# Sandwich layer on eight cores: the PSUM eviction of y moved from VectorE to ScalarE, and the first FFN block placed between the last transposes

## The reference

```python
x = u
# diagonal state space model, 32 complex states
Bu  = einsum('bld,nd->bln', layernorm(x), B_bar)
xs  = scan(a=Lam_bar, b=Bu)                  # over the 4096 tokens
y   = 2*real(einsum('bln,dn->bld', xs, C)) + D * layernorm(x)
x   = x + layernorm(y)
# quantised feed-forward, hidden size 5632, uint8 weights minus 128, times a scale
h   = silu(layernorm(x) @ Wg.T) * (layernorm(x) @ Wu.T)
out = x + layernorm(h @ Wd.T)
```

## Time and profile before

| | us |
|---|---|
| median of 3 runs | 2667.18 |
| lowest, highest run | 2664.41, 2741.41 |
| the profiled execution, time | 2664.85 |
| the profiled execution, span of its slowest core (core 5) | 2663.3 |
| spans of the eight cores | 2651.8 to 2663.3 |

### The profile page before, as it was taken

How to read it: one execution, slowest core, us unless ns; L and a number is a source line. 1 busy time by engine, 2 the same in 40 slices (tenths; PEclk the granted TensorE clock), 3 DMA queues, 4 the chain that set the end, 5 groups by cost and what they waited for, 6 DMA issues and landing times.

```text
span 2663.3 us, 26373 instructions; the slowest of 8 cores (2651.8 to 2663.3 us)
## 1 busy us (share of the span) xinstructions
PE 2111.1 (79%) x10668; PEld 1024.1 (38%) x10668; DVE 758.5 (28%) x1412; ACT 497.2 (19%) x465; POOL 126.6 (5%) x238
## 2 busy tenths in 40 slices
PE   1466224332999999999978979999999999998980
PEld 0455212221444444444433434444444444443330
DVE  5666686764111111111011012221222221011114
ACT  1454202233100000000412210000000003122201
POOL 1000000001000000000000000000000000000000
PEclk9877655565999999999988989999999999999995
DMA  2344013335122122223222122333333323121216
GB/s 64 132 153 159 16 63 127 126 127 157 65 79 79 67 77 79 80 79 148 109 97 93 48 107 80 126 114 123 127 127 127 122 84 134 44 95 73 80 49 221
DMA packets 51579, 270.20 MB, mean 101 GB/s; under 512 B 6146, under 2 KB 6146, under 8 KB 34818
## 3 DMA queue, kind: packets, MB, share of 16 engines
q0 software_dynamic: 30528, 146.81, 15.6%
q1 hardware_dynamic: 20356, 117.51, 12.8%
q10 hardware_dynamic: 576, 4.19, 0.4%
HBM read 151.58 MB, written 47.71 MB: 75 GB/s over the span
## 4 chain that ended last, share of the span: by engine, by line
PE 76%; DVE 13%; DMA 4%; issue 4%; ACT 2%; DVEq 0%; SPq 0%; POOL 0%; ACTq 0%; POOLq 0%
PE pA L751 12%; PE pA L788 12%; PE pA L761 11%; PE pB L751 11%; PE pB L788 6%; PE pD L761 6%; PE pC L761 6%; PE pD L788 3%; PE pC L788 3%; DVE arena L936 2%; DVE arena L1095 1%; DVE arena L1082 1%; DMA out<-arena 1%; DVE arena L1076 1%; DMA ysp<-arena 1%
## 5 line engine op out<-in xcount | busy, mean ns | idle before, releaser
L788 PE MATMUL pA<-arena 128*128 128x512 bf16 x1408 | 373.8, 386 | 22.4 <-DVE arena L1187 18.9
L751 PE MATMUL pA<-arena 128*128 128x512 bf16 x1408 | 316.3, 383 | 17.8 <-DMA arena<-wu 13.4
L761 PE MATMUL pA<-arena 128*128 128x512 bf16 x1408 | 311.1, 379 | 0.0
L751 PE MATMUL pB<-arena 128*128 128x512 bf16 x1408 | 311.1, 379 | 0.0
L788 PE MATMUL pB<-arena 128*128 128x512 bf16 x704 | 215.8, 387 | 30.7 <-DVE arena L1187 30.7
L788 PEld LDWEIGHTS pA<-arena 128*128 128x128 bf16 x1408 | 139.4, 99 | 199.6 <-issue 41.7
L751 PEld LDWEIGHTS pA<-arena 128*128 128x128 bf16 x1408 | 138.6, 99 | 188.4 <-issue 25.4
L1151 DVE TENSOR_SCALAR arena<-pA,arena 128x512 bf16<-128x512 f32 x88 | 62.0, 746 | 500.0 <-PE pA L761 500.0
L700 PE MATMUL pA<-arena 32*128 32x512 bf16 x64 | 39.4, 616 | 207.3 <-DVE arena L1095 136.7
L751 PEld LDWEIGHTS pB<-arena 128*128 128x128 bf16 x1408 | 138.0, 98 | 165.9
L761 PEld LDWEIGHTS pA<-arena 128*128 128x128 bf16 x1408 | 137.8, 98 | 166.1
(11 more groups left out here) (202 smaller groups left out, 1714.2 us busy)
## 6 DMA issues: line engine op xcount, KB each, us to landing
arena<-wg POOLq DMA_DIRECT2D x88, 512.0 KB, 3.5
arena<-wu POOLq DMA_DIRECT2D x88, 512.0 KB, 4.3
arena<-u SPq DMA_DIRECT2D x32, 1024.0 KB, 6.0
arena<-wd POOLq DMA_DIRECT2D x16, 1408.0 KB, 5.9
arena<-wd POOLq DMA_DIRECT2D x8, 2816.0 KB, 10.0
arena<-uprev SPq DMA_DIRECT2D x16, 1024.0 KB, 5.7
x1sp<-arena SPq DMA_DIRECT2D x16, 1024.0 KB, 4.7
arena<-x1sp SPq DMA_DIRECT2D x16, 1024.0 KB, 10.0
```

The costliest lines, as they stand in the source:

```text
L751: C.inc(t.matmul(gps[tg], wgbuf[par][:, kt * 128:(kt + 1) * 128], xnt[:, kt * TH + tg * 512: kt * TH + (tg + 1) * 512], start=(kt == 0), s ...
L761: C.inc(t.matmul(ups[tg], wubuf[par][:, kt * 128:(kt + 1) * 128], xnt[:, kt * TH + tg * 512: kt * TH + (tg + 1) * 512], start=(kt == 0), s ...
L788: C.inc(t.matmul(PS2[ti], Hbuf[:, hb * TH + ti * 128: hb * TH + (ti + 1) * 128], wsrc[:, wof * 512:(wof + 1) * 512], start=(hb == 0), stop ...
```

## The change

Three edits.

- ACT copies `pA` to `ybuf_p`, at the head of its slot, and DVE only waits for that (`yev_k`) ahead of the y statistics. The copy waited for `ln2_(k-2)` before; it waits for `x1_(k-2)` now.
- POOL issues the weight loads of the first two blocks ahead of the spill stores. Each waits for the y matmuls that read the SBUF range below it.
- PE does block hb 0 of X 0 in four groups of 16 matmuls, one behind each of the transposes of tiles 11 to 14. Block hb 1 is the first in the loop over blocks.

```diff
--- before.py
+++ after.py
@@ -417,6 +417,15 @@
                                   channel_multiplier=1), "g",
                   mark=("g_ddiag" if kd == 15 else None))
 
+        for hb in (0, 1):
+            wkey = "d_w" if hb % 2 == 0 else "d_w2"
+            C.wait(g, f"ymm_{11 + hb}")
+            C.inc(g.dma_start(wgbuf[hb][:, :], d_in["wg"][hb, :, :]),
+                  wkey, 16)
+            C.wait(g, f"ymm_{13 + hb}")
+            C.inc(g.dma_start(wubuf[hb][:, :], d_in["wu"][hb, :, :]),
+                  wkey, 16, mark=f"wconv_0_{hb}")
+
         for k in range(8):
             C.wait(g, f"xnevv_{k + 8}")
             C.wait(g, f"xnevs_{k + 8}")
@@ -429,12 +438,11 @@
 
         for X in range(2):
             for hb in range(HB):
+                if X == 0 and hb < 2:
+                    continue
                 par = hb % 2
-                if X == 0 and hb < 2:
-                    C.wait(g, "yev_15")
-                else:
-                    pX, phb = (X, hb - 2) if hb >= 2 else (0, HB - 2 + hb)
-                    C.wait(g, f"s1mm_{pX}_{phb}")
+                pX, phb = (X, hb - 2) if hb >= 2 else (0, HB - 2 + hb)
+                C.wait(g, f"s1mm_{pX}_{phb}")
                 wkey = "d_w" if par == 0 else "d_w2"
                 C.inc(g.dma_start(wgbuf[par][:, :], d_in["wg"][hb, :, :]),
                       wkey, 16)
@@ -533,6 +541,15 @@
                            bias=c_Tlnr), "s", mark="s_rpow")
         for sl in range(NT + 5):
             k = sl - 1
+            if 0 <= k < NT:
+                C.wait(s, f"ymm_{k}")
+                if k >= 2:
+                    C.wait(s, f"x1_{k-2}")
+                for gq in range(4):
+                    C.inc(s.activation(
+                        ybuf_p[k % 2][:, 512 * gq:512 * (gq + 1)],
+                        pA[:, 512 * gq:512 * (gq + 1)], AF.Copy), "s",
+                        mark=(f"yev_{k}" if gq == 3 else None))
             if 0 <= k < NT:
                 C.wait(s, f"yaggr_{k}")
                 C.inc(s.activation(sdy_p[k % 2], mvy_p[k % 2][:, 1:2],
@@ -714,17 +731,39 @@
                       mark=(f"ymm_{i}" if kd == 15 else None))
             if i >= 5:
                 xntr_block(i - 5)
-        for k in range(NT - 5, NT):
-            xntr_block(k)
+        def s1q0(buf, ps, tg, mk):
+            for kt in range(16):
+                C.inc(t.matmul(ps,
+                               buf[:, kt * 128:(kt + 1) * 128],
+                               xnt[:, kt * TH + tg * 512:
+                                   kt * TH + (tg + 1) * 512],
+                               start=(kt == 0), stop=(kt == 15)), "t",
+                      mark=(mk if kt == 15 else None))
+
+        xntr_block(11)
+        C.wait(t, "wconv_0_0")
+        C.wait(t, "yev_15")
+        C.wait(t, "xnevv_3")
+        C.wait(t, "xnevs_3")
+        s1q0(wgbuf[0], pA[:, 0:512], 0, None)
+        xntr_block(12)
+        C.wait(t, "xnevv_7")
+        C.wait(t, "xnevs_7")
+        s1q0(wgbuf[0], pA[:, 512:1024], 1, "gmm_0_0")
+        xntr_block(13)
+        s1q0(wubuf[0], pA[:, 1024:1536], 0, None)
+        xntr_block(14)
+        s1q0(wubuf[0], pA[:, 1536:2048], 1, "s1mm_0_0")
+        xntr_block(15)
 
         PS2 = [pA[:, 0:512], pA[:, 512:1024], pA[:, 1024:1536],
                pA[:, 1536:2048], pB[:, 0:512], pB[:, 512:1024], pC, pD]
         for X in range(2):
             for hb in range(HB):
+                if X == 0 and hb == 0:
+                    continue
                 par = hb % 2
                 C.wait(t, f"wconv_{X}_{hb}")
-                if X == 0 and hb == 0:
-                    C.wait(t, "yev_15")
                 if X == 0 and hb == 1:
                     C.wait(t, "xnevv_15")
                     C.wait(t, "xnevs_15")
@@ -1087,15 +1126,7 @@
                       mark=f"x1aggr_{k}")
             k = sl - 1
             if 0 <= k < NT:
-                C.wait(v, f"ymm_{k}")
-                if k >= 2:
-                    C.wait(v, f"ln2_{k-2}")
-                C.selfwait(v, "v")
-                for gq in range(4):
-                    C.inc(v.tensor_copy(
-                        ybuf_p[k % 2][:, 512 * gq:512 * (gq + 1)],
-                        pA[:, 512 * gq:512 * (gq + 1)]), "v",
-                        mark=(f"yev_{k}" if gq == 3 else None))
+                C.wait(v, f"yev_{k}")
                 C.selfwait(v, "v")
                 for gq in range(4):
                     C.inc(v.bn_stats(
```

## The result

The changed kernel takes 2599.88 us (median of 8 runs, 2597.14 to 2603.54). The ratio to the kernel before is 0.9753, 95% interval 0.9739 to 0.9768: 2.5% faster, where 2604.3 us and 2.36% were forecast.

What follows compares the result with a forecast made beforehand. A ring of waits in the tile loop, 17.33 us a turn, was taken as the bound. 8.0 + 33.8 - 4.7 + 25.25 - 0.6 - 1.2 = 60.5 us saved from 2664.85 gave 2604.3 us, range 2593 to 2626.

Steps and rivals of the forecast that it cites:

- first slots: Start of the tile loop, up to tile 4's eviction: shorter without the wait behind x1 statistics, gain 8.0 us.
- eleven turns: Tile loop from there to the last y eviction: 191.1 us becomes 157.3 at 14.3 a turn, gain 33.8.
- tail: Transposes, evictions and spill stores after the last y eviction: first ACT steps start later, loss 0.6 us.
- half clock at the start of hb 1: PE's clock may have dropped before block hb 1: cost between 0 and 2.5 us, 1.2 taken.
- E: Time of the y eviction on ACT, four f32 PSUM copies: 2.12 to 2.54 us, 2.35 taken.
- The ring: Tile loop's ring of waits: PE, normalise on ACT, add on DVE, evict on ACT; 17.33 us falls to 14.3 a turn.
- The spill: Tile 8's spill queues on POOL behind the early weight loads and delays tile 9's evictions: loss 4.7 us once.
- the rival that had them exposed: Tail: the four matmul blocks between the last transposes stay uncovered, costing 27.3 us, total 2632; chance 0.10.
- Clock up in the loop: Rival: PE keeps its clock in the tile loop, the statistics ring of 13.4 sets the turn: 2593 us; chance 0.10.
- Table loads: Rival: ACT reloads its function table around the eviction, four loads a turn cost 72 us: 2676 us; chance 0.02.
- The rate of ACT: ACT time per element: page's 0.833 ns would make four copies 1.7 us; the trace's 1.02 ns was used.
- Longer turns: Rival: engines and DMA meet more often in the tile loop; turns of 16 us lose 19: 2623 us; chance 0.12.

Runs made afterwards that it cites:

- e1: Kernel before with only the y eviction moved to ACT, weights and first block as before: 2618.1 us, ratio 0.9821 to the kernel before.
- e3: Changed kernel with the y eviction kept on DVE, right behind the x1 add and ahead of the x1 statistics: 2625.2 us, ratio 0.9848.
- e5: Changed kernel with the spill of tile 8 ahead of block hb 1's weight loads on POOL: 2596.6 us, ratio 0.9736.
- e2: Changed kernel with the y eviction back on DVE as before, keeping early weights and block pieces: 2647.9 us, ratio 0.9932.
- e4: Changed kernel with block hb 0 in one piece behind the last transposes, weights still early: 2608.7 us, ratio 0.9783.
- e7: On top of e6 and e5, ACT does xnapply and its pB eviction right behind the y eviction: 2564.3 us, ratio 0.9615.
- e6: Changed kernel with PE doing the transposes of tile i-5 before y of tile i: 2589.3 us, ratio 0.9709.
- e8: On top of e7, block hb 1 does its up half before its gate half: 2558.5 us, ratio 0.9612.

## Where the prediction held, and which of its terms failed

By its own terms, in us, from the profiled executions (66.8 between them, 60.5 forecast):

| term | forecast | trace |
|---|---|---|
| start of the loop (another core is the slowest) | 0 | +0.7 |
| first slots, to the end of tile 4's eviction | +8.0 | +9.5 |
| eleven turns, with the wait for the spill | +33.8 - 4.7 = +29.1 | +33.8 |
| weights and first block | +25.25 | +25.2 |
| tail | -0.6 | -1.6 |
| half clock at the start of hb 1 | -1.2 | -2.2 |
| sum (of the unrounded terms), at the start of block hb 2 | 60.5 | 65.3 |

The other 1.5 of the 66.8 lies behind the start of stage 2, where nothing was changed. The mechanism was the forecast one; what failed is the size of terms. The loop was priced 6.2 us too low (first slots and turns), and the tail and the half clock cost 2.0 more than forecast. That these partly cancel, so that the time came out within 4.4 us of the forecast and inside its range of 2593 to 2626, is luck.

- **The step that failed is E,** the term of the sum for the eviction on ACT. I took 2.35 us, the middle between 2.12 (bf16 evictions) and 2.54 (SiLU from f32 PSUM). It measured 2.06, below the lower bound, so it was wrong to take four bf16 evictions as the least that four f32 ones can take. Why the f32 ones are not the slower stays open. That is 0.3 in each turn, 3.2 of the 4.7 us that the eleven turns gave beyond the forecast. Most of the rest is the clock below, and 0.1 to 0.4 the spill.
- **The first slots:** 0.9 of the 1.5 us was there before the add of tile 0. I had left that add where it was before, though the two evictions ahead of it are 0.4 us shorter each. The rest is within what E gives in three evictions.
- **The ring** was right, in its members and in what is late next. Turns began at 14.05 to 14.25 and fell to 13.7 from tile 10 on: the transposes shortened from 1.91 to 1.54 us, since the clock went up before they were over, and this is what the turns lost. The turns of before fell in the same way (17.65 to 17.0). e1 and e3 show the ring: with all of DVE's copies kept, moving the eviction ahead of the statistics alone gives 15.48.
- **The spill** behind POOL's wait: forecast 4.7, measured 4.3 to 4.6 in the changed kernel (18.15 against the 13.8 of the turn ahead of it, and 13.6 in e5 and e1) and 4.7 in e2. e5 takes it away.
- **The tail** was forecast 0.6 longer and is 1.6 longer. The 0.6 is there (0.57 in e1). What I had put at nothing are the two stores: 0.7 for the one that lands later beside the pieces, 0.36 for the one that POOL issues later (see e4).
- **The pieces are hidden,** but for that store: the rival that had them exposed, 27.3 us and 2632, is out. No piece delayed a transpose. The block in one piece behind the transposes costs 7.4 us by the rows (e4).
- **The half clock:** I took half of 2.5; it was 2.2, nearly all. PE rested 5.7 us between the transposes of tile 15 (606.60 + 1.05) and block hb 1 at 613.3. My figure of 2 to 4 us was too short: it took the fourth piece and the transposes at half clock, and much of both ran at full clock and was over earlier; and the last eviction came 1.0 us later than forecast.
- **Clock up in the loop** (2593): not in that form. The mean clock of the loop, from the first y to the last y eviction, rose from 0.55 to 0.57. Each y still began at 1.2 GHz (0.50 in the rows), and only the transposes gained.
- **Table loads:** ACT does one, 1.28 us at its first root of y (375.92), as before the change (377.06), and none in the turns that follow. Four copies and a root stand behind each other without one. The Trainium skill ("ScalarE: Activation LUTs", Table sets: the hidden batching unit) has copy and identity in every set, and the trace agrees.
- **The rate of ACT:** I had left out a part of what the Trainium skill says. Beside the 0.833 ns per element, "ScalarE: Activation LUTs" (What ACT_TABLE_LOAD costs) gives a fixed time for each instruction: 186 ns with immediate scale and bias, some 93 ns of which overlap between instructions that follow each other. An estimate from these figures is 0.61 us for a copy of 512 elements and 2.17 us for four in a row. The trace has a median of 0.601 us for one and 2.06 us for four, so the page fits them to about 5%, and the 1.7 us of the prediction was not what it gives.
- **Longer turns** by DMA: 2 MB now move in 13.9 us, and in e7 in 11.6, without an add that waited for a load.

## What to carry to other kernels

Where no engine is full, write out the ring of waits and ask of each member whether it must stand there. Here the y eviction stood behind statistics that nobody in the ring needed; taking it out and giving it to ACT was worth 48 us. A turn took 17.4 us before, 15.5 with the eviction still on DVE but in the better place, and 13.9 with it on ACT: a little over half of the gain is the place, the rest the engine. Then compute the next ring at once: it tells whether a further exchange of two operations in an engine's order pays, as it did twice here. Check its members in the timeline even when the sum comes out right. And when a load is issued early on an in-order queue, look at what is queued behind its wait.

## What the runs showed that I had not expected

- Four f32 evictions of 128 x 512 from PSUM took 2.06 us on ACT and 2.48 us on DVE; four bf16 ones on ACT 2.12 by two pairs. The wider type was not slower to read.
- PE's rest ahead of a block matters: after 5.7 us of rest the first 32 matmuls of block hb 1 took 9.1 us (613.3 to 622.45) against 6.9 at full clock. In e2, e3, e5 and e6, with the same rest of 5.7 us, they took 9.2, 8.4, 9.7 and 8.8; so the length of the rest alone does not tell the cost. In e8 PE rested 2.9 us, did the transposes of tile 15 and went straight on: the first 16 took 4.3 us (572.73 to 576.98) against 3.46.
- As turns went on, PE's clock rose before the transposes were over, in both kernels: they took 1.91 us at first and at the least 1.45 after the change, 1.49 before it.
